# Relational layers of a graph network: groups of 20 edge tiles with 6 picked, through a ring of six one-hot pieces

## The chip, the core and the metric

The kernel runs on one core of one Trainium2 chip. The metric is the device time of one execution in microseconds. Most executions of one kernel agree within 0.3%.

## The reference, cut to what matters

Four layers of a graph network run one after the other on 3125 nodes of 32 features and 53125 edges that are sorted by destination. The change touches the first, which is two relational layers in a row. Each edge has one of 20 types, and the weights of a type are a mixture of 8 basis matrices:

```python
def _rel_layer(x, src, dst, etypes, V, a, w_loop, bias, activation=None):
    W = jnp.einsum('rb,bio->rio', a, V)
    seg = dst.astype(jnp.int32) * R + etypes.astype(jnp.int32)
    agg = jax.ops.segment_sum(x[src], seg, num_segments=N * R)
    agg = agg.reshape(N, R, -1)
    h = jnp.einsum('nri,rio->no', agg, W) + x @ w_loop + bias
    if activation is not None:
        h = activation(h)
    return h
...
h = _rel_layer(x, src, dst, etypes, V1, a1, loop1, b1, activation=jax.nn.relu)
h = _rel_layer(h, src, dst, etypes, V2, a2, loop2, b2, activation=None)
...
edge_index = jnp.stack([src, dst])
h = jnp.maximum(_layernorm(x, axis=-1), 0.0)
x = x + _L0_gnn_ref(h, src, dst, edge_type_20, ...)
```

So the output of a node is the sum of the messages of its incoming edges, and the message of an edge is the source's feature row times the matrix of the edge's type. The sum layer, the flow layer and the attention layer follow.

## The kernel before

The edges lie in `T` = 440 tiles of 128 edges; all edges of a tile end in one block of 128 nodes, of which there are `NB` = 25. `add_up_pass` (L680) is called once for each relational layer; both calls are alike but for a prologue of the first, and each is called a pass here. A pass adds the messages of all tiles into `rel_acc`, which lies in PSUM, a block's 32 columns at a time. A tile is added by one matmul in fp32 (two passes of the array, so two records in a trace): the stationary operand is the tile's destination one-hot (`rel_onehot`, 128 edges by 128 nodes), the moving one its 128 messages of 32 features.

The messages of a tile come in one of two ways. **Gathered** tiles: GpSimd (POOL) issues one indirect DMA a tile (L732), which fetches 128 rows from `message_table` in HBM, where the messages of all pairs of node and type stand. **Picked** tiles are computed on the core: VectorE (DVE) compares the tiles' source numbers, a row broadcast to all partitions (`rel_sources`), with the node numbers of one block, a chunk (L795), and so makes the chunk's part of the source one-hot (`rel_source_onehot`, in bf16); TensorE (PE) multiplies these one-hots with the node features in three bf16 parts (L870) and sums over the 25 chunks, which gives the source's features (`p_rel_picked`); ScalarE (ACT) copies them to SBUF; PE multiplies them with the eight basis matrices (L897, the basis products, into `p_rel_terms`); DVE weighs the eight terms with the coefficients of the edge's type (L812, `weigh`) and adds them up (L821, `messages`); PE adds the result like a gathered tile (`picked_messages`). The coefficients come from a small matmul (L887) with a one-hot of the types (L804).

The tiles go in groups of `RG` = 11, the last `RPT` = 3 of them picked, so there are 40 groups a pass, 8 gathers a group. Nothing but the written order of the code and its semaphores sets the order of the work; every engine runs its list in order.

- PE, a group: `pick` (25 matmuls of 384 columns, L870), `gathered_messages` (8 tiles, L861), `coefficients` (L887), `picked_messages` of the group two back (L861), `basis_products` (L897).
- DVE, a group: five stretches of five chunks' comparisons of 384 columns (L795), with two or three tiles' destination one-hots (L782) between them, then `weigh` of the group two back (L812), `types` (L804) and `messages` of the group two back (L821). The source one-hots of a whole group have two buffers, so DVE starts group g when PE has picked group g-2.
- POOL: the gathers, with six groups of row buffers; group g waits until PE has added group g-6.
- SP: the broadcasts of source and type numbers of the picked tiles (L755), six groups ahead.

## Time and profile before

| | us |
|---|---|
| median of 3 runs (lowest, highest) | 3623.91 (3616.06, 3626.77) |
| the profiled execution | 3605.4 |
| its span | 3603.6 |
| first pass, PE's first pick to its last matmul | 651.65 to 1102.4 |
| second pass, DVE's first comparison to PE's last matmul | 1176.4 to 1630.9 |
| TensorE's granted clock over the span, share of full | 0.807 |

A profile shows for each engine when it was busy, and for each idle stretch what ended it (the releaser). "issue" as a releaser means that the engine waited for nothing that the profile shows: POOL spends about 0.30 us so between two gathers. The granted clock is the share of its full 2.4 GHz that TensorE's clock had in a stretch; a single stretch has either 1.0 or 0.5 (1.2 GHz), and a mean over longer windows lies between. "PEld" is the load of a stationary operand, which goes beside the matmuls.

### The profile page before, as it was taken

To read this page: it belongs to the slowest core of one execution; us is meant where nothing else is said; L and a number is where in the kernel's file an instruction comes from. 1 tells how busy PE (TensorE), PEld (TensorE's weight loads), DVE (VectorE), ACT (ScalarE), POOL (GpSimd) and SP (SyncE) were. 2 spreads that over 40 slices of the span, in tenths; PEclk is the share of its full clock that TensorE was granted. 3 is DMA by queue.
4 is the path that set the end of the run, shared out by engine and by line. 5 is a ranking of instruction groups with operands and counts; after the bars stand their busy time and mean duration, and the time that the engine had idled before them with its cause. 6 is when DMAs were issued, how large, how long until landed. Compare 5 with 4: busy or idle time off the path is not lost. (4 is left out here: it accounts for less than half of the span.)

```text
span 3603.6 us, 57390 instructions
## 1 busy us (share of the span) xinstructions
PE 2602.2 (72%) x19362; PEld 1786.6 (50%) x19499; DVE 2548.7 (71%) x7445; ACT 576.6 (16%) x1352; POOL 2289.0 (64%) x2253
## 2 busy tenths in 40 slices
PE   0600000899998999996999799999999967777761
PEld 0300000777775777774666466666666544333331
DVE  9400000988983988878999777777777659999987
ACT  0100000000001000000111122222222213333320
POOL 2777776877770777775777455555555357777740
PEclk9655555778885788887999799999999969888875
DMA  6300001111113111111111100000000011111120
GB/s 97 104 8 8 8 8 58 31 22 23 24 15 100 25 23 23 23 13 29 29 29 29 13 10 10 10 10 11 10 11 10 6 24 27 27 27 27 27 18 5
DMA packets 125024, 91.60 MB, mean 25 GB/s; under 512 B 59542, under 2 KB 110678, under 8 KB 124118
## 3 DMA queue, kind: packets, MB, share of 16 engines
q0 software_dynamic: 70912, 41.10, 9.2%
q1 hardware_dynamic: 53846, 46.89, 5.7%
q8 instruction: 174, 2.85, 0.3%
q14 instruction: 92, 0.75, 0.1%
HBM read 60.42 MB, written 27.41 MB: 24 GB/s over the span
## 5 line engine op out<-in xcount | busy, mean ns | idle before, releaser
L732 POOL DMA_INDIRECT rel_rows<-message_table,message_indices x640 | 716.3, 1119 | 279.2 <-issue 194.4
L1287 POOL DMA_INDIRECT flow_x<-node_table,flow_index x440 | 443.1, 1007 | 401.2 <-DVE flow_index L1302 292.2
L1425 PE MATMUL flow_acc_bwd<-flow_onehot_j,flow_by_q 128*128 128x309 bf16 (+1 forms) x2503 | 552.2, 334 | 8.9 <-issue 0.2
L795 DVE TENSOR_SCALAR rel_source_onehot<-rel_sources,node_numbers 128x384 bf16<-128x384 f16 x2000 | 508.1, 315 | 62.6 <-PE p_rel_picked L870 61.4
L393 POOL DMA_INDIRECT sorted_edges<-stage,sorted_row x416 | 404.8, 973 | 191.9 <-issue 126.5
L1653 POOL DMA_INDIRECT att_kv_rows<-kv_table,att_index x440 | 424.0, 964 | 140.6 <-issue 129.8
L870 PE MATMUL p_rel_picked<-rel_source_onehot,rel_h_parts 128*96 128x384 bf16 x2000 | 429.4, 384 | 0.4 <-DVE rel_source_onehot L795 0.4
L870 PEld LDWEIGHTS p_rel_picked<-rel_source_onehot,rel_h_parts 128*96 128x96 bf16 x2000 | 297.0, 149 | 122.1 <-issue 0.7
L664 PE MATMUL p_rel_terms<-ident,source_centred 128*128 128x128 f32 (+1 forms) x4 | 1.1, 436 | 455.8 <-DVE source_centred L650 455.8
L1036 POOL DMA_INDIRECT sum_rows<-node_table,src_indices x280 | 271.2, 968 | 85.2 <-issue 85.2
L761 DVE COPY p_rel_lanes<-iota 128x128 f32<-128x128 f32 x2 | 0.6, 294 | 440.1 <-PEq L388 437.5
L1689 DVE TENSOR_REDUCE att_tile_max<-p_att_scores 128x4 f32<-128x512 f32 x440 | 282.3, 684 | 25.5 <-PE p_att_scores L1803 21.5
L1070 DVE TENSOR_SCALAR sum_source_onehot<-sum_sources,node_numbers 128x512 bf16<-128x512 f16 x1000 | 299.3, 365 | 0.0
L1123 PE MATMUL p_sum_picked<-sum_source_onehot,sum_h_stack 128*96 128x512 bf16 x1000 | 250.5, 413 | 34.5 <-DVE sum_source_onehot L1070 33.9
L1801 PE MATMUL p_att_scores<-att_mask,identb 128*128 128x512 bf16 x440 | 197.7, 449 | 67.0 <-ACT att_parts_turned L1737 67.0
L1422 PE MATMUL flow_acc_fwd<-flow_messages,flow_onehot 128*128 128x32 bf16 x1320 | 235.1, 178 | 1.5 <-DVE flow_by_q L1330 1.5
L664 PEld LDWEIGHTS p_rel_terms<-ident,source_centred 128*128 128x128 f32 (+1 forms) x4 | 0.7, 203 | 457.1 <-DVE source_centred L650 457.1
L1315 DVE TENSOR_TENSOR flow_messages<-p_hidden,flow_b 128x256 f32<-128x256 f32 x110 | 46.7, 425 | 245.8 <-PE p_hidden L1413 245.8
L844 ACT CAST rel_picked<-p_rel_picked 96x384 bf16<-96x384 f32 x80 | 38.0, 474 | 1101.5 <-PE p_rel_picked L870 1101.5
L1330 DVE TENSOR_TENSOR flow_by_q<-flow_messages,source_q_mask 128x512 bf16<-128x512 bf16 x330 | 207.3, 681 | 0.0
L861 PE MATMUL rel_acc<-rel_rows,rel_onehot 128*128 128x32 f32 x1280 | 166.3, 287 | 54.2 <-DMA rel_rows<-message_table,message_indices 53.9
L1803 PE MATMUL p_att_scores<-att_parts_turned,att_pick 96*128 96x512 bf16 x440 | 201.5, 458 | 0.0
(286 smaller groups left out, 4979.9 us busy)
## 6 DMA issues: line engine op xcount, KB each, us to landing
message_table<-message_rows SPq DMA_DIRECT2D x50, 320.0 KB, 2.1
rel_rows<-message_table,message_indices POOLq DMA_INDIRECT x640, 2.7
rel_sources<-source_rows SPq DMA_DIRECT2D x80, 96.0 KB
flow_x<-node_table,flow_index POOLq DMA_INDIRECT x440, 2.4
att_kv_rows<-kv_table,att_index POOLq DMA_INDIRECT x440, 2.5
sorted_edges<-stage,sorted_row POOLq DMA_INDIRECT x416, 2.1
sum_sources<-source_rows SPq DMA_DIRECT2D x40, 128.0 KB, 3.2
sum_rows<-node_table,src_indices POOLq DMA_INDIRECT x280, 2.4
```

Of the source, the lines that this page charges most:

```text
L393: pool.indirect_dma_start(out=d["sorted"], out_offset=bass.IndirectOffsetOnAxis(ap=row[:, c:c + 1], axis=0), in_=stage[:, c, :], in_offset ...
L732: pool.indirect_dma_start(out=rows[b][:, t, :], out_offset=None, in_=d["messages"], in_offset=bass.IndirectOffsetOnAxis(ap=s["idx_msg"][:, ...
L795: last = dve.tensor_scalar(which[g % 2][:, c, :], srcs[b][:], s["node"][:, c:c + 1], None, ALU.is_equal)
L870: last = pe.matmul(pp[g % 2][0:3 * F, 0:RW], hs[:, c].rearrange("p k f -> p (k f)"), which[g % 2][:, c, :], start=(c == 0), stop=(c == NB ...
L1036: pool.indirect_dma_start(out=rows[b][:, t, :], out_offset=None, in_=d["nodes"], in_offset=bass.IndirectOffsetOnAxis(ap=s["idx_src"][:, g ...
L1070: last = dve.tensor_scalar(which[g % 2][:, c, :], srcs[g % bufs][:], node[:, c:c + 1], None, ALU.is_equal)
L1123: last = pe.matmul(pp[g % 2][0:3 * F, 0:PT * P], hs[:, c].rearrange("p k f -> p (k f)"), which[g % 2][:, c, :], start=(c == 0), stop=(c == ...
L1287: pool.indirect_dma_start(out=X[b][:, t, 0:F], out_offset=None, in_=d["nodes"], in_offset=bass.IndirectOffsetOnAxis(ap=ibuf[b][:, t:t + 1] ...
L1422: pe.matmul(accF[:, bass.ds(cols[b, t], F)], hot[b][:, t, :], top(M[b][:])[:, k, t, 0:F], start=False, stop=True, skip_group_check=True)
L1425: last = pe.matmul(accB[:, lo:hi], S[b][:, t, k, :], J[b][:, t, lo:hi], start=False, stop=True, skip_group_check=True)
L1653: pool.indirect_dma_start(out=KV[b][:, t, :], out_offset=None, in_=d["kv"], in_offset=bass.IndirectOffsetOnAxis(ap=ibuf[b][:, t:t + 1], ax ...
L1689: dve.tensor_reduce(tm[b][:, 0, t, :], pR[t % PR][:].rearrange("p (h e) -> p h e", h=HEADS), AX_X, ALU.max).then_inc(max_ready, 1)
```

## The change

The groups become 20 tiles, 6 of them picked (22 groups a pass, 14 gathers a group; 308 gathered and 132 picked tiles instead of 320 and 120). One comparison now makes a chunk's one-hots of all six picked tiles, 768 columns. The source one-hots of a group no longer lie in one of two large buffers but go through a ring of six pieces (`SLOTS`) of five chunks each (`PIECE`), a fifth of a group. PE picks piece by piece, two matmuls of 384 columns for each chunk with the same stationary operand, into two PSUM buffers that are the two halves (`HALF` = 3 tiles) of the group. Basis products, weighing and adding up go half by half. Row buffers are 3 of 14 tiles instead of 6 of 8. The order on PE and DVE is written anew: all that PE does for a group besides picking (additions, basis products) now stands one group later, between the five picks of the next group, and DVE's `weigh` and `messages` stand one group later, after the second and the fourth piece.

```diff
-RG, RPT, RBUFS = 11, 3, 6
+RG, RPT, RBUFS = 20, 6, 3
+HALF = RPT // 2
...
+PIECE, SLOTS = NB // FIFTHS, 6
...
-            which = [sb(st1, f"{name}_source_onehot{b}", [P, NB, RW], BF16) for b in range(2)]
+            which = [sb(st1, f"{name}_source_onehot{b}", [P, PIECE, RW], BF16) for b in range(SLOTS)]
...
-            gT = [sb(st1, f"{name}_picked{b}", [3 * F, RW], BF16) for b in range(2)]
+            gT = [sb(st1, f"{name}_picked{b}", [3 * F, HALF * P], BF16) for b in range(2)]
...
-            terms = sb(st1, f"{name}_terms", [P, RPT, F, NBASIS])
-            msg = [sb(st1, f"{name}_messages{b}", [P, RPT, F]) for b in range(2)]
+            terms = sb(st1, f"{name}_terms", [P, HALF, F, NBASIS])
+            msg = [sb(st1, f"{name}_messages{b}", [P, HALF, F]) for b in range(2)]
...
+                    def sources(g, n):
+                        piece = g * FIFTHS + n
+                        if n == 0:
+                            dve.wait_ge(edge_in[g % RBUFS], 32 * (g // RBUFS) + 32)
+                        if piece >= SLOTS:
+                            dve.wait_ge(piece_used, piece - SLOTS + 1)
+                        for c in range(PIECE):
+                            last = dve.tensor_scalar(which[piece % SLOTS][:, c, :], srcs[g % RBUFS][:],
+                                                     s["node"][:, n * PIECE + c:n * PIECE + c + 1], None, ALU.is_equal)
+                        last.then_inc(piece_ready, 1)
...
+                    def weigh(g, x):
+                        dve.wait_ge(z_done, 2 * g + x + 1)
                         dve.wait_ge(coef_taken, g + 1)
+                        if g + x >= 1:
+                            dve.wait_ge(msg_ready, 2 * g + x)
...
-                    for g in range(RGROUPS):
+                    for g in range(RGROUPS + 1):
                         for n in range(FIFTHS):
-                            sources(g, n * NB // FIFTHS, (n + 1) * NB // FIFTHS)
-                            if n < FIFTHS - 1:
+                            if g < RGROUPS:
+                                sources(g, n)
+                            if n in (1, 3) and g >= 1:
+                                weigh(g - 1, n // 2)
+                            if n < FIFTHS - 1 and g < RGROUPS:
                                 onehots(g, n * RG // (FIFTHS - 1), (n + 1) * RG // (FIFTHS - 1))
-                        if g >= 2:
-                            weigh(g - 2)
-                        types(g)
-                        if g >= 2:
-                            messages(g - 2)
...
+                            if n in (1, 3) and g >= 1:
+                                messages(g - 1, n // 2)
+                            if n == 2 and g < RGROUPS:
+                                types(g)
...
+                    def pick(g, n):
+                        piece = g * FIFTHS + n
+                        pe.wait_ge(piece_ready, piece + 1)
+                        if n == 0 and g >= 1:
+                            pe.wait_ge(pick_taken, 2 * g)
+                        for c in range(PIECE):
+                            for x in range(2):
+                                last = pe.matmul(pp[x][0:3 * F, 0:HALF * P],
+                                                 hs[:, n * PIECE + c].rearrange("p k f -> p (k f)"),
+                                                 which[piece % SLOTS][:, c, x * HALF * P:(x + 1) * HALF * P],
+                                                 start=(n + c == 0), stop=(n * PIECE + c == NB - 1))
+                        last.then_inc(piece_used, 1)
...
-                    for g in range(RGROUPS):
-                        pick(g)
-                        gathered_messages(g)
-                        coefficients(g)
+                    for g in range(RGROUPS + 2):
+                        now, before = g < RGROUPS, 1 <= g <= RGROUPS
                         if g >= 2:
                             picked_messages(g - 2)
-                        basis_products(g)
-                    picked_messages(RGROUPS - 2)
-                    picked_messages(RGROUPS - 1)
+                        if before:
+                            columns(g - 1)
+                            gathered_messages(g - 1, 0, RGT // 2)
+                        if now:
+                            pick(g, 0)
+                        if before:
+                            basis_products(g - 1, 0)
+                        if now:
+                            pick(g, 1)
+                            pick(g, 2)
+                        if before:
+                            basis_products(g - 1, 1)
+                        if now:
+                            pick(g, 3)
+                            coefficients(g)
+                        if before:
+                            gathered_messages(g - 1, RGT // 2, RGT)
+                        if now:
+                            pick(g, 4)
```

PE's list, before, from the picks of one group to those of the next (`rel1_moved5` is the landing of the gathers; rows of the same addition are left out):

```order
L870 MATMUL p_rel_picked<-rel_source_onehot,rel_h_parts 96x384 [waits rel1_pick_taken,rel1_source_onehot_ready]
L870 MATMUL p_rel_picked<-rel_source_onehot,rel_h_parts 96x384 x24
L860 ISA [waits rel1_moved5,rel1_onehot_ready]
...
L887 MATMUL p_rel_coef<-rel_type_coef,rel_type_onehot 128x8 [waits rel1_coef_taken,rel1_type_onehot_ready]
L887 MATMUL p_rel_coef<-rel_type_coef,rel_type_onehot 128x8 x2
L860 ISA [waits rel1_messages_ready]
...
L897 MATMUL p_rel_terms<-rel_basis_parts,rel_picked 128x256 [waits rel1_terms_taken,rel1_pick_taken]
L897 MATMUL p_rel_terms<-rel_basis_parts,rel_picked 128x256 x8
L84 TENSOR_LOAD dst_columns
```

PE's list now, from the second pick of a group to the last additions of the group before (`rel1_source_onehot_ready` counts pieces, `rel1_terms_taken` DVE's weighings):

```order
L871 MATMUL p_rel_picked<-rel_source_onehot,rel_h_parts 96x384 [waits rel1_source_onehot_ready]
L871 MATMUL p_rel_picked<-rel_source_onehot,rel_h_parts 96x384 x9
L871 MATMUL p_rel_picked<-rel_source_onehot,rel_h_parts 96x384 [waits rel1_source_onehot_ready]
L871 MATMUL p_rel_picked<-rel_source_onehot,rel_h_parts 96x384 x9
L901 MATMUL p_rel_terms<-rel_basis_parts,rel_picked 128x256 [waits rel1_terms_taken,rel1_pick_taken]
L901 MATMUL p_rel_terms<-rel_basis_parts,rel_picked 128x256 x8
L871 MATMUL p_rel_picked<-rel_source_onehot,rel_h_parts 96x384 [waits rel1_source_onehot_ready]
L871 MATMUL p_rel_picked<-rel_source_onehot,rel_h_parts 96x384 x9
L891 MATMUL p_rel_coef<-rel_type_coef,rel_type_onehot 128x8 [waits rel1_coef_taken,rel1_type_onehot_ready]
L891 MATMUL p_rel_coef<-rel_type_coef,rel_type_onehot 128x8 x5
L860 ISA [waits rel1_moved0,rel1_onehot_ready]
```

The picks stood in one block with one wait ahead of them; now each fifth has its own wait, and basis products and additions stand between the fifths.

DVE's list, before, the end of a group and the start of the next:

```order
L795 TENSOR_SCALAR rel_source_onehot<-rel_sources,node_numbers 128x384 x5
L812 TENSOR_TENSOR rel_terms<-p_rel_terms,rel_coef 128x768 [waits rel1_messages_ready,rel1_coef_taken,rel1_terms_done]
L804 TENSOR_SCALAR rel_type_onehot<-rel_types,lane_number 20x384 [waits rel1_coef_done,rel1_edge_rows_in4]
L821 TENSOR_REDUCE rel_messages<-rel_terms 128x96 [waits rel1_used,rel1_terms_taken]
L795 TENSOR_SCALAR rel_source_onehot<-rel_sources,node_numbers 128x384 [waits rel1_pick_done,rel1_edge_rows_in5]
```

DVE's list now, from the second piece of a group to its third and the fourth:

```order
L796 TENSOR_SCALAR rel_source_onehot<-rel_sources,node_numbers 128x768 [waits rel1_source_onehot_used]
L796 TENSOR_SCALAR rel_source_onehot<-rel_sources,node_numbers 128x768 x4
L811 TENSOR_TENSOR rel_terms<-p_rel_terms,rel_coef 128x768 [waits rel1_messages_ready,rel1_coef_taken,rel1_terms_done]
L783 TENSOR_TENSOR rel_onehot<-p_rel_lanes,dst_in_block 128x640
L820 TENSOR_REDUCE rel_messages<-rel_terms 128x96 [waits rel1_used,rel1_terms_taken]
L796 TENSOR_SCALAR rel_source_onehot<-rel_sources,node_numbers 128x768 [waits rel1_source_onehot_used]
L796 TENSOR_SCALAR rel_source_onehot<-rel_sources,node_numbers 128x768 x4
L783 TENSOR_TENSOR rel_onehot<-p_rel_lanes,dst_in_block 128x640
L803 TENSOR_SCALAR rel_type_onehot<-rel_types,lane_number 20x768 [waits rel1_coef_done]
```

The weighing, which waits for PE's basis products (`rel1_terms_done`), stood behind all of a group's comparisons; now it stands twice among them, and the third piece is made behind the first of the two.

## Rows read from the trace of the kernel before

**Rows 1.** The stretches of the two passes: busy time by engine, granted clock.

```profile
core 0: us, PE busy (x) PEld busy (x) DVE busy (x) ACT busy (x) POOL busy (x), PEclk, DMA share, GB/s
643.00:1097.00 454.00, 425.86 (x2502) 344.74 (x2503) 394.60 (x1278) 26.10 (x80) 349.09 (x305) 0.80 0.17 22
1182.00:1631.00 449.00, 420.36 (x2468) 337.70 (x2466) 381.40 (x1236) 26.11 (x80) 337.76 (x308) 0.80 0.16 21
```

**Rows 2.** Who waited for whom in the first pass: total us, times, longest.

```profile
POOL rel_rows L732 <- issue: 93.6, 307, 0.3
DVE rel_terms L812 <- PE p_rel_terms L897: 34.8, 7, 15.1
...
PE rel_acc L861 <- DMA rel_rows<-message_table,message_indices: 27.2, 13, 4.0
DVE rel_source_onehot L795 <- PE p_rel_picked L870: 25.6, 11, 3.9
```

**Rows 3.** Costliest groups of the whole page: busy us, mean ns | idle before.

```profile
L732 POOL DMA_INDIRECT rel_rows<-message_table,message_indices x640 | 716.3, 1119 | 279.2 <-issue 194.4
L1287 POOL DMA_INDIRECT flow_x<-node_table,flow_index x440 | 443.1, 1007 | 401.2 <-DVE flow_index L1302 292.2
...
L1036 POOL DMA_INDIRECT sum_rows<-node_table,src_indices x280 | 271.2, 968 | 85.2 <-issue 85.2
```

**Rows 4.** PE in order of time, picks at full clock: start, us, operation, count.

```profile
1187.57 4.23 PE L870 MATMUL p_rel_picked<-rel_source_onehot,rel_h_parts 128*96 128x384 bf16 x25
1191.64 1.87 PE L861 MATMUL rel_acc<-rel_rows,rel_onehot 128*128 128x32 f32 x16
```

**Rows 5.** PE in order of time, the small matmuls between two groups of picks.

```profile
1249.40 1.87 PE L861 MATMUL rel_acc<-rel_rows,rel_onehot 128*128 128x32 f32 x16
1251.20 0.83 PE L887 MATMUL p_rel_coef<-rel_type_coef,rel_type_onehot 20*128 20x8 f32 x6
1251.96 0.86 PE L861 MATMUL rel_acc<-rel_messages,rel_onehot 128*128 128x32 f32 x6
1252.65 1.25 PE L897 MATMUL p_rel_terms<-rel_basis_parts,rel_picked 96*128 96x256 bf16 x9
1253.69 2.77 PE L870 MATMUL p_rel_picked<-rel_source_onehot,rel_h_parts 128*96 128x384 bf16 x8
```

**Rows 6.** PE in order of time, additions after a wait for gathers.

```profile
1216.25 3.62 PE L861 MATMUL rel_acc<-rel_rows,rel_onehot 128*128 128x32 f32 x16 [4.13 <-DMA rel_rows<-message_table,message_indices]
```

**Rows 7.** Granted clock in three stretches; columns as in the first group.

```profile
1209.30:1226.30 17.00, 12.87 (x62) 10.57 (x61) 15.71 (x51) 0.65 (x2) 13.65 (x12) 0.70 0.11 17
1226.30:1236.50 10.20, 10.20 (x65) 8.30 (x64) 7.33 (x26) 0.65 (x2) 7.76 (x9) 0.83 0.21 26
1236.60:1243.30 6.70, 6.70 (x52) 5.88 (x51) 6.70 (x22) 0.65 (x2) 5.18 (x6) 1.00 0.23 29
```

**Rows 8.** DVE and POOL in order of time, one group of the second pass.

```profile
1411.97 0.54 DVE L782 TENSOR_TENSOR rel_onehot<-p_rel_lanes,dst_in_block 128x384 f32<-128x384 f32 x1
1412.44 1.22 DVE L795 TENSOR_SCALAR rel_source_onehot<-rel_sources,node_numbers 128x384 bf16<-128x384 f16 x5
1412.71 1.76 POOL L732 DMA_INDIRECT rel_rows<-message_table,message_indices  x1 [0.30 <-issue]
1413.58 0.94 DVE L812 TENSOR_TENSOR rel_terms<-p_rel_terms,rel_coef 128x768 f32<-128x768 f32 x1
1414.45 0.40 DVE L804 TENSOR_SCALAR rel_type_onehot<-rel_types,lane_number 20x384 f32<-20x384 f16 x1
1414.77 0.93 DVE L821 TENSOR_REDUCE rel_messages<-rel_terms 128x96 f32<-128x768 f32 x1
```

**Rows 9.** Three comparisons: duration min/median/max ns, first and last start, forms.

```profile
L795 DVE TENSOR_SCALAR rel_source_onehot<-rel_sources,node_numbers x2000: 294/306/550, 643.4 to 1601.7; 128x384 bf16<-128x384 f16 x182
L1070 DVE TENSOR_SCALAR sum_source_onehot<-sum_sources,node_numbers x1000: 332/341/551, 1649.8 to 2005.4; 128x512 bf16<-128x512 f16 x167
L1309 DVE TENSOR_SCALAR flow_onehot_j<-iota_j,source_j x440: 419/430/614, 2045.9 to 2859.0; 128x821 bf16<-128x821 f16 x147
```

97 lines of the change are left out of this document (35 added, 62 removed).

## The prediction, written before the changed kernel had run

> **What bounds the kernel now.** I read the busy time of the two passes first [rows 1]. In each pass of some 450 us PE is busy 94% of the time, DVE 85 to 87%, POOL 75 to 77%; ACT does not matter. But busy shares mislead twice here. POOL's share leaves out the 0.30 us between two gathers: its only idle time in the pass is that one, "issue", 307 times [rows 2], so POOL never waits for anybody. 320 gathers at a mean of 1.119 us [rows 3] and 0.30 us make 454 us, which is the length of a pass: **the gathers set the pace**. And PE's 94% is at a granted clock of 0.80. PE still waits for the gathers, 27.2 us in 13 waits, and DVE waits for PE, 25.6 us for picks and 34.8 us for basis products (15 us of it once, at the end) [rows 2]. So three engines are nearly balanced, POOL a little ahead of the others.
>
> PE's own work is best counted at full clock. From start to start of rows [rows 4, 5]: 25 picks 4.07 us (0.163 each), 8 additions 1.80, coefficients 0.76, three picked messages 0.69, basis products 1.04: **8.36 us a group**. At 0.80 that is 10.45, and 40 groups make 418; PE was busy 426 [rows 1], so small gaps add 2% (factor 1.02). With the 28 us that PE is idle it is the 454 of the row. This is the formula that I use for after: work at full clock, times 1.02, over the clock, plus idle time.
>
> The clock itself is set by what PE does. It falls after the small matmuls (few columns, 4.3 us in a row [rows 5]) and comes back in the picks: a group without a wait runs at 0.83, its picks and additions at 1.00 in between [rows 7]. Where PE also waits for gathers, 4.13 us at 1216.25, the additions after it run at half clock (3.62 us against 1.87) [rows 5, 6], and that stretch of 17 us has a mean of 0.70 [rows 7].
>
> **POOL after.** 12 gathers a pass go: 12 x 1.42 = 17 us. Beside that I expect shorter gathers. A gather in these passes can stretch far over its neighbours' length, as the one of 1.76 us that starts in a run of five comparisons and ends in the weighing behind it [rows 8]. The same gather takes 0.968 us on average beside comparisons of 512 columns, and 1.007 beside those of 821 [rows 3, 9]. The new ones have 768, between the two, so 0.99: 308 x 1.29 = 397 us instead of 454. That is a gain of 57 us a pass on the engine that bounds now, and it is what could be had, if PE and DVE can follow.
>
> The Trainium skill speaks against it: "SBUF — State Buffer", section "SBUF: two separate sides", says that VectorE in a two-port mode holds a port pair for its whole instruction and that GpSimd, which writes descriptors for its gathers through it, blocks fully. By that, comparisons twice as long would lengthen the gathers, and the sum for POOL would rise above 454 instead of falling to 397. The rows of the sum and flow layers speak against that reading; it stands below as a rival.
>
> **DVE after.** The shortest comparison takes 294 ns at 384 columns, 332 at 512, 419 at 821 [rows 9]: 0.28 ns a column, so 404 ns at 768. Five of 384 take 1.22 us [rows 8], which is a start every 0.23 us, some 65 ns less than the duration; at 768 that is 0.34 us, **1.70 us a piece**. Before: 40 x 25 x 0.23 = 230 us a pass; after: 22 x 5 x 1.70 = 187. Destination one-hots: three tiles 0.47 us from start to start [rows 8]; five, at 0.135 more a tile, 0.74; four a group. Weighing 0.87 and adding up 0.86 keep their size of three tiles and come twice a group; types 0.7 (0.32 from start to start for 384 [rows 8], about twice that for 768). A group: 8.5 + 3.0 + 3.5 + 0.7 = 15.7 us, 345 a pass, against 380 before. DVE gains 35 us a pass.
>
> **PE after.** 50 picks 8.15 us, 14 additions 3.15, coefficients 1.52, six picked messages 1.38, basis products 2.08: **16.3 us a group**, 358 a pass at full clock against 334. The two picks of a chunk use the same stationary operand; the list shows a load for each, and loads hide behind matmuls now, so nothing is gained or lost. The load of 20 column numbers now stands between picked messages and additions; before, no idle time shows where it stands [rows 5], and 1.38 us of matmuls cover it, so I take 0 and bound it at 0.4 us a group.
>
> **The new order makes a wait.** DVE's first weighing in a group stands behind two pieces and waits for PE's first basis products; behind the waiting DVE stands piece 2 of the same group. PE, once those basis products are done, has only one fifth of picks (10 x 0.163 = 1.6 us at full clock, 3.2 at half) before it needs that piece. DVE must first weigh (0.87), make one-hots (0.74), add up (0.86) and make the piece (1.70), with some 0.1 for POOL's interference and 0.4 for two semaphore hops: 4.7 us. **PE stands idle 4.7 - 1.6 = 3.1 us, or 1.5 when the picks ran at half clock; I take 2.8**, once in each of 21 groups: 59 us a pass. The ring of six pieces does not help, for it is the weighing and not the ring that holds DVE: DVE has two pieces of the group made, PE has used one. After the second basis products PE has a long list without DVE (picks, coefficients, additions, picks, messages, additions, picks, basis products: 12 us at full clock) in which DVE does its remaining 9 us and then waits some 4 to 8 us. So the two wait for each other in turns, and POOL, freed, ends up waiting for row buffers.
>
> Before, the weighing stood behind all comparisons and was two groups late, and such waits were 34.8 us a pass in all on DVE and none on PE.
>
> **The clock after.** A group has two stretches of small matmuls of 3.1 us (less than the 4.3 of before) and one idle stretch of some 3 us. Between a group without idle time, 0.83, and one with it, 0.70 [rows 7], I take the middle: **0.77**. Pass: 22 x 16.3 x 1.02 / 0.77 = 475, idle 59, and 5 for the end, where half a group more is left after the last gather: **539 us, against 454**: +85 a pass, +170 for both. Against the profiled execution's 3605.4 that is 3775. The median of the three runs, 3623.91, is 18.5 above the profiled one, so the forecast for the median is **3794**. I see no effect on the other layers.
>
> Bounds: with a clock of 0.83 and an idle time of 1.5 a pass takes 441 + 32 + 5 = 478, +24, and the kernel 3672; with 0.70, 3.1 and 0.4 for the column load, 522 + 65 + 5 + 9 = 601, +147, and 3918. Both ends need two things to go the same way, so I keep within them.
>
> **Rivals.**
> 1. *The clock stays up, and the change is faster.* The small matmuls are cut into shorter stretches between picks; for it speaks that picks restore the clock at once [rows 7]. At 1.00 a group takes 16.6 + 3.1 = 19.7 us, a pass 433 + 5 = 438, -16: 3592. It decides from a mean clock of about 0.94 (22 x 16.6 / 0.94 + 59 + 5 = 452). Against it: each group now has an idle stretch, and the one row of before with such a stretch shows 0.70. Chance 0.09.
> 2. *Gathers get longer, not shorter*, as the skill's rule on the port pair would have it. If each took the 1.76 us of the long one [rows 8], POOL would need 308 x 2.06 = 634 us a pass, it would set the pace with some 180 us more a pass, 3980. The means beside 512 and 821 columns speak against it [rows 3]. Chance 0.03.
> 3. *PE does not idle*, because DVE gets ahead after all and the wait falls where PE is busy: 475 + 5 = 480, +26 a pass, 3676. The list of the changed DVE speaks against it. Chance 0.07.
> 4. *The freed gathers and the new waits cancel*: a clock of 0.90 to 0.94. 3613 to 3635. Chance 0.03.
>
> My forecast has 0.78. The range 3690 to 3860 holds the middle of it and leaves out rival 1, 2, most of 3 and the far ends. A measurement of this kernel can tell 0.3% (11 us) from no change. Slower by more: 0.78 + 0.03 + 0.07 = 0.88; within: 0.03; faster: 0.09.
>
> **What would show it.** In the changed profile: PE waiting for `rel_source_onehot`, about 21 times 3 us a pass, where before it waited for gathers; DVE's waits for basis products, 34.8 us a pass before, up to 130 us or more; POOL with waits for `rel_rows` to be used, some 100 us a pass, and gathers near 0.99 us; comparisons near 0.40 us; a granted clock of 0.74 to 0.80 in both passes; passes of about 540 us. I would be wrong if the clock stays over 0.9 (then about no change or faster), if PE's waits for pieces are under 1 us, or if POOL still shows no wait.

## The result and the profile of the changed kernel

| | before | changed |
|---|---|---|
| median (lowest to highest), us | 3619.98 (3603.87 to 3626.77) | 3659.68 (3653.99 to 3667.53) |
| profiled execution: span, us | 3603.6 | 3661.4 |
| mean granted clock over the span | 0.807 | 0.824 |

The ratio is 1.0129, with a 95% interval of 1.0100 to 1.0158. The change is slower, as forecast, but by 40 us where 170 were forecast, and 3659.68 lies under the range 3690 to 3860.

The two profiled executions differ by 57.8 us. The first pass ends with its last addition at 1120.3 us instead of 1102.4, the second at 1676.4 instead of 1630.9, so 45.5 us are gone by then. The other 12 lie in the layers behind, whose code is the same: from the end of the second pass the profiled execution of before needs 1972.7 us, that of the changed kernel and those of experiments 1 to 4 need 1983.5 to 1987.1.

The two passes of the changed kernel, as [rows 1] has them of before (there the first stretch ends 5 us ahead of the end of its pass; stretch and length, then busy time and instructions of PE, PEld, DVE, ACT and POOL, then granted clock, DMA share and GB/s):

```profile
643.00:1121.00 478.00, 418.57 (x2682) 335.50 (x2681) 340.36 (x750) 23.11 (x66) 320.26 (x293) 0.88 0.14 21
1196.80:1677.00 480.20, 420.65 (x2644) 334.58 (x2643) 332.52 (x731) 23.11 (x66) 328.56 (x299) 0.87 0.13 20
```

PE has 24 us more work a pass (at full clock) and yet is busy 12 us less in the first pass than before (430.3 us, counted to the last addition), since its clock is 0.88, not 0.80. The loss stands in the other part of the pass: PE is idle for 59 us in place of 29. Who waited for whom in the first pass (total, times, longest), to be read beside [rows 2]:

```profile
PE p_rel_picked L871 <- DVE rel_source_onehot L796: 56.7, 21, 2.8
PE p_rel_terms L901 <- DVE rel_terms L811: 1.1, 1, 1.1
PE rel_acc L861 <- DVE rel_messages L820: 0.6, 1, 0.6
...
DVE rel_terms L811 <- PE p_rel_terms L901: 134.5, 39, 8.9
...
POOL rel_rows L733 <- issue: 87.7, 277, 1.9
POOL rel_rows L733 <- PE rel_acc L861: 36.8, 16, 6.6
```

PE no longer waits for gathers in this pass; it waits for a piece of one-hots, once in each of 21 groups. DVE waits for basis products, and POOL, which never waited before, waits for row buffers. The two groups of the page that answer to [rows 3, 9]:

```profile
L733 POOL DMA_INDIRECT rel_rows<-message_table,message_indices x616 | 674.2, 1095 | 347.5 <-issue 182.8
...
L796 DVE TENSOR_SCALAR rel_source_onehot<-rel_sources,node_numbers 128x768 bf16<-128x768 f16 x1100 | 380.1, 411 | 0.8 <-DMA rel_types<-type_rows 0.6
```

One group of the second pass in order of time (start, us, operation, count, idle time before it):

```profile
1271.22 1.50 PE L891 MATMUL p_rel_coef<-rel_type_coef,rel_type_onehot 20*128 20x8 f32 x12
...
1272.65 1.75 PE L861 MATMUL rel_acc<-rel_rows,rel_onehot 128*128 128x32 f32 x14
1274.23 1.81 PE L871 MATMUL p_rel_picked<-rel_source_onehot,rel_h_parts 128*96 128x384 bf16 x10
...
1281.37 1.79 PE L871 MATMUL p_rel_picked<-rel_source_onehot,rel_h_parts 128*96 128x384 bf16 x10
1281.57 0.96 DVE L811 TENSOR_TENSOR rel_terms<-p_rel_terms,rel_coef 128x768 f32<-128x768 f32 x1 [3.76 <-PE p_rel_terms L901]
1282.44 0.82 DVE L783 TENSOR_TENSOR rel_onehot<-p_rel_lanes,dst_in_block 128x640 f32<-128x640 f32 x1
1283.17 0.94 DVE L820 TENSOR_REDUCE rel_messages<-rel_terms 128x96 f32<-128x768 f32 x1
1284.03 1.73 DVE L796 TENSOR_SCALAR rel_source_onehot<-rel_sources,node_numbers 128x768 bf16<-128x768 f16 x5
...
1285.82 2.42 PE L871 MATMUL p_rel_picked<-rel_source_onehot,rel_h_parts 128*96 128x384 bf16 x10 [2.66 <-DVE rel_source_onehot L796]
...
1288.03 2.13 PE L901 MATMUL p_rel_terms<-rel_basis_parts,rel_picked 96*128 96x256 bf16 x9
```

DVE weighs, makes destination one-hots, adds up and only then makes the piece that PE needs; PE has run out of picks meanwhile and stands for 2.66 us. That is the wait of the forecast, step for step. The clock of the same group, in two stretches with the columns of [rows 1]:

```profile
1269.18:1285.50 16.32, 13.97 (x102) 11.62 (x100) 12.32 (x27) 1.05 (x3) 12.42 (x13) 0.98 0.16 29
1285.80:1291.20 5.40, 5.38 (x26) 3.76 (x27) 3.87 (x9) 0.00 (x0) 4.49 (x4) 0.68 0.08 11
```

For 16.3 of the group's 20.6 us, with the additions and coefficients in it, PE is at 0.98. In this group the half clock comes once, behind the idle time, and falls on picks and basis products (2.42 us for ten picks against 1.79). It isn't so in every group. In the one before, the clock also falls where PE had waited for nothing since 1240.87, and additions and picked messages run at half of it (3.17 us for 14 additions against 1.73):

```profile
1248.54 2.64 PE L871 MATMUL p_rel_picked<-rel_source_onehot,rel_h_parts 128*96 128x384 bf16 x10
1250.97 2.61 PE L861 MATMUL rel_acc<-rel_messages,rel_onehot 128*128 128x32 f32 x12
1253.40 3.17 PE L861 MATMUL rel_acc<-rel_rows,rel_onehot 128*128 128x32 f32 x14
```

### The profile page after: what moved, and what is told of

The parts are those of the page before. It is cut to its first block and busy times, and to the rows that moved or that the text cites. A ratio compares the mean times of both kernels' runs of the same rounds, so it can differ in the third digit from the quotient of the medians.

```text
span 3661.4 us, 56571 instructions
## 1 busy us (share of the span) xinstructions
PE 2594.0 (71%) x19682; PEld 1769.7 (48%) x19819; DVE 2437.9 (67%) x6381; ACT 570.5 (16%) x1324; POOL 2246.8 (61%) x2229
## 5 line engine op out<-in xcount | busy, mean ns | idle before, releaser
L733 POOL DMA_INDIRECT rel_rows<-message_table,message_indices x616 | 674.2, 1095 | 347.5 <-issue 182.8
L871 PE MATMUL p_rel_picked<-rel_source_onehot,rel_h_parts 128*96 128x384 bf16 x2200 | 460.1, 364 | 114.3 <-DVE rel_source_onehot L796 113.8
L871 PEld LDWEIGHTS p_rel_picked<-rel_source_onehot,rel_h_parts 128*96 128x96 bf16 x2200 | 287.7, 136 | 227.7 <-DVE rel_source_onehot L796 132.7
L796 DVE TENSOR_SCALAR rel_source_onehot<-rel_sources,node_numbers 128x768 bf16<-128x768 f16 x1100 | 380.1, 411 | 0.8 <-DMA rel_types<-type_rows 0.6
L1707 DVE TENSOR_REDUCE att_tile_max<-p_att_scores 128x4 f32<-128x512 f32 x440 | 283.2, 684 | 25.1 <-PE p_att_scores L1821 20.6
L811 DVE TENSOR_TENSOR rel_terms<-p_rel_terms,rel_coef 128x768 f32<-128x768 f32 x88 | 84.2, 957 | 278.6 <-PE p_rel_terms L901 278.2
L841 ACT COPY rel_coef<-p_rel_coef 128x48 f32<-128x48 f32 x44 | 8.7, 198 | 1249.0 <-PE p_rel_coef L891 1249.0
```

The source lines that it names most:

```text
L733: pool.indirect_dma_start(out=rows[b][:, t, :], out_offset=None, in_=d["messages"], in_offset=bass.IndirectOffsetOnAxis(ap=s["idx_msg"][:, ...
L796: last = dve.tensor_scalar(which[piece % SLOTS][:, c, :], srcs[g % RBUFS][:], s["node"][:, n * PIECE + c:n * PIECE + c + 1], None, ALU.is_ ...
L871: last = pe.matmul(pp[x][0:3 * F, 0:HALF * P], hs[:, n * PIECE + c].rearrange("p k f -> p (k f)"), which[piece % SLOTS][:, c, x * HALF * P ...
L1707: dve.tensor_reduce(tm[b][:, 0, t, :], pR[t % PR][:].rearrange("p (h e) -> p h e", h=HEADS), AX_X, ALU.max).then_inc(max_ready, 1)
```

## Experiments

Four kernels ran on one chip; the kernel before had a median of 3607.23 us there.

### 1. Both orders rewritten so that PE never needs a fresh piece (e1_no_idle)

The two lists stand here by the names of their calls, not as code.

```diff
 # DVE, one group: the order of the calls
-sources 0, onehots, sources 1, weigh 0, onehots, messages 0, sources 2, onehots, types,
-sources 3, weigh 1, onehots, messages 1, sources 4
+sources 0, onehots, sources 1, onehots, types, sources 2, weigh 0, onehots, messages 0,
+sources 3, onehots, weigh 1, sources 4, messages 1
 # PE, one group
-picked messages, gathered 0, pick 0, basis 0, pick 1, pick 2, basis 1, pick 3,
-coefficients, gathered 1, pick 4
+gathered 0, pick 0, basis 0, picked messages, pick 1, pick 2, coefficients, basis 1,
+pick 3, gathered 1, pick 4
```

> The changed kernel with another order on DVE and PE, same work: DVE weighs after the third and the fourth piece instead of after the second and the fourth, types stand one place earlier, and PE puts picked messages and coefficients between the picks and the second basis products. Theory A (the wait of PE for the third piece, 57 us a pass, is what the changed kernel loses): that wait falls under 10 us a pass, the passes shrink from 478 to about 440, where 308 gathers of 1.40 us (431 us) are the bound, and the kernel takes 3580 to 3605 us. Rival B (the ten per cent more picks on PE are what it loses): the idle time only moves, and the time stays within 15 us of the changed kernel's 3660.

Measured: 3582.59 us, ratio 0.9931 (0.9911 to 0.9952), as theory A had it; rival B falls. By the ratios it beats both kernels. Its passes and the waits of the first:

```profile
643.00:1081.00 438.00, 396.44 (x2687) 327.55 (x2687) 344.33 (x751) 23.14 (x66) 328.93 (x294) 0.91 0.14 23
1157.00:1597.00 440.00, 392.07 (x2645) 319.70 (x2644) 335.00 (x731) 23.14 (x66) 332.44 (x300) 0.91 0.14 22
...
PE rel_acc L878 <- DMA rel_rows<-message_table,message_indices: 41.0, 15, 6.5
...
POOL rel_rows L733 <- issue: 89.3, 293, 0.3
```

No wait for a piece is left, POOL waits for nobody, and the pass is 308 gathers x (1.12 + 0.30) = 438 us: the gathers set the pace again. So the larger groups were worth 22 us in this pass (459.4 us before, counted from 643 to the last addition, and 437.4 here), and the written order of DVE and PE hid it. What this run can't say is which of the two orders did it, nor whether the clock (0.91 for 0.88) came from the waits for pieces, which are gone, or from PE's order.

### 2. All fourteen additions in one place (e2_one_stretch)

```diff
-gathered_messages(g - 1, 0, RGT // 2)   # ahead of pick 0
 ...
-gathered_messages(g - 1, RGT // 2, RGT) # ahead of pick 3
+gathered_messages(g - 1, 0, RGT)        # behind the picked messages
```

> The changed kernel with all 14 gathered tiles of a group added in one place, right behind the picked messages, instead of in two halves. Theory C (TensorE's clock stays up in the changed kernel, 0.88 against 0.80, because the small matmuls are cut into short stretches with picks between them): the stretch of small matmuls becomes 4.5 us, the mean clock of the passes falls to 0.82 or less, PE is busy some 30 us a pass longer, and the kernel takes 3700 to 3730 us. Rival D (the clock is up because PE no longer waits for gathers right beside its small matmuls): clock 0.87 to 0.88 and the time within 15 us of 3660.

Measured: 3762.72 us, ratio 1.0436 (1.0397 to 1.0475). The first pass, its waits, and PE in one group:

```profile
643.00:1174.00 531.00, 447.22 (x2690) 353.63 (x2690) 344.72 (x752) 23.14 (x66) 313.49 (x294) 0.84 0.12 19
...
PE p_rel_picked L871 <- DVE rel_source_onehot L796: 80.2, 48, 2.9
...
DVE rel_terms L811 <- PE p_rel_terms L901: 182.4, 31, 12.6
...
1306.18 2.61 PE L861 MATMUL rel_acc<-rel_messages,rel_onehot 128*128 128x32 f32 x12
1308.60 6.16 PE L861 MATMUL rel_acc<-rel_rows,rel_onehot 128*128 128x32 f32 x28
1314.58 3.41 PE L871 MATMUL p_rel_picked<-rel_source_onehot,rel_h_parts 128*96 128x384 bf16 x10
```

In this group the same additions take 6.16 us in one row of 28 matmuls, all at half clock, where two rows of 14 take 1.75 and 1.73 at full clock in the group shown of the changed kernel. The clock of the pass fell from 0.88 to 0.84 and PE was busy 29 us a pass longer. Theory C holds in its direction, with two misses: I had expected a lower clock still, 0.82 or less, and less loss in time, 3700 to 3730 us. The time has a second part, waits on both sides that grew by 24 us (PE) and 48 us (DVE) a pass, because a long row of additions also holds up the basis products that DVE waits for.

### 3. The kernel before, with its picks cut in two (e3_before_split)

The waits stay ahead of the first part, and the signal that the picks are done stays behind the second.

```diff
-                        pick(g)
+                        pick(g, 0, 13)
                         gathered_messages(g)
+                        pick(g, 13, NB)
                         coefficients(g)
```

> The kernel before with one edit on PE: the 25 picks of a group are cut in 13 and 12, and the additions of the gathered tiles stand between them. Theory C (short stretches of small matmuls keep the clock up): the mean clock of the passes rises from 0.80 to 0.87 or more. Since gathers set the pace before (no wait on POOL), the time stays within 0.5% of before even so, and PE waits for gathers longer, 27 to 60 us a pass. Rival D: the clock stays at 0.80, since the waits for gathers stay.

Measured: 3633.19 us, ratio 1.0088 (1.0060 to 1.0115). The same stretch of this kernel and then of the kernel before:

```profile
700.00:1080.00 380.00, 334.30 (x2060) 265.73 (x2059) 329.36 (x1071) 21.54 (x66) 299.40 (x265) 0.86 0.14 21
...
700.00:1080.00 380.00, 356.78 (x2100) 287.17 (x2099) 336.06 (x1083) 22.19 (x68) 298.06 (x269) 0.81 0.15 21
```

PE has 2% fewer instructions in it and is busy 22 us (6%) less, at 0.86 in place of 0.81, since the small matmuls no longer stand in one row. PE's waits for gathers rose from 27.2 to 48.2 us a pass and the clock rose all the same. The kernel is no faster, for PE isn't what sets its pace. It is 0.9% slower, where I had expected a difference within 0.5%, and the clock missed the expected 0.87 narrowly; what costs the 26 us isn't shown (the gathers are 0.012 us longer on average, 8 us in all).

Whether idle time lowers the clock stands in the traces. The table has the time at half clock in the first pass, from its first pick to its last addition, in us and with the number of stretches. A stretch counts as behind a wait when it begins during an idle time of PE of over 0.8 us or within 2.5 us of its end.

| kernel | at half clock | behind a wait | no wait ahead |
|---|---|---|---|
| before | 178 | 101 (12) | 76 (22) |
| this one, picks cut | 123 | 116 (17) | 7 (2) |
| changed | 103 | 55 (16) | 49 (9) |
| changed, additions joined (experiment 2) | 155 | 60 (10) | 95 (20) |
| changed, both orders rewritten (experiment 1) | 69 | 66 (10) | 3 (1) |

So both lower it. Cutting the picks took away nearly all the half clock that no wait preceded (76 us, then 7; with a limit of 2.0 us, 97 and then 14), and joining the additions doubled it: that part is the order's. The other part follows waits, and it is the larger one in this kernel and in experiment 1. From the kernel before to the changed one both parts fell, so rival D of experiment 2 has a share too; how large it is depends on the limit (47 us of 75 with 2.5 us, 26 with 2.0).

### 4. The kernel before with seven gathers a group (e4_seven_gathers)

The eighth gather of a group is left out, and its tile is added up from the seventh's rows.

```diff
-                        for t in range(RGT):
+                        for t in range(RGT - 1):
                             pool.indirect_dma_start(
```

> The kernel before with work left out: seven gathers a group instead of eight, and the eighth tile is added from the rows of the seventh, so PE and DVE do the same as before. Theory G (the gathers set the pace before): 280 gathers of 1.42 us are 398 us, PE's 418 to 426 us at its clock become the bound, the passes shrink by 20 to 30 us each and the kernel takes 3560 to 3585 us. Rival (PE is the bound already): within 10 us of before.

Measured: 3548.87 us, ratio 0.9839 (0.9799 to 0.9879), 58 us less, and 11 less than the lowest that theory G had. The gathers' group, beside [rows 3]:

```profile
L732 POOL DMA_INDIRECT rel_rows<-message_table,message_indices x560 | 680.8, 1216 | 253.8 <-issue 170.1
```

POOL was busy 35.5 us less (716.3 before) and had 80 gaps of 0.30 us fewer, 24 us: 59.5 together, which is the whole gain. So the gathers did set the pace before. But 80 gathers fewer, by the 1.42 us of the forecast, should have freed 114 us. The rest became longer (1.216 us): 146 of 560 take over 1.3 us, where it was 117 of 640. DVE's comparisons come faster now, in a first pass of 419 us instead of 451, and may hold more of them; that they do isn't shown.

### 5. One order at a time, and shorter runs of comparisons

Three more kernels were to settle what was left. The first has e1's DVE order alone, the second its PE order alone, the third is e1 with one tile of destination one-hots behind each comparison of pieces 0 to 3:

```diff
                             last = dve.tensor_scalar(which[piece % SLOTS][:, c, :], srcs[g % RBUFS][:],
                                                      s["node"][:, n * PIECE + c:n * PIECE + c + 1], None, ALU.is_equal)
-                        last.then_inc(piece_ready, 1)
+                            if c == PIECE - 1:
+                                last.then_inc(piece_ready, 1)
+                            if spread:
+                                onehots(g, FIFTHS * n + c, FIFTHS * n + c + 1)
```

In all runs of this section, those of the kernel before too (medians 4253 to 4305 us), engines stood between instructions for which nothing was waited, so ratios count here only within the section, and no time is compared with the sections ahead. A trace shows it where the first pass begins (the kernel with DVE's order alone, third run):

```profile
683.93 0.42 DVE L796 TENSOR_SCALAR rel_source_onehot<-rel_sources,node_numbers 128x768 bf16<-128x768 f16 x1 [0.98 <-issue]
683.95 0.21 PE L978 MATMUL rel_acc<-w_loop,h_transposed 33*128 33x32 f32 x1 [2.59 <-issue]
...
685.33 0.42 DVE L796 TENSOR_SCALAR rel_source_onehot<-rel_sources,node_numbers 128x768 bf16<-128x768 f16 x1 [0.98 <-issue]
...
686.05 0.21 PE L978 MATMUL rel_acc<-w_loop,h_transposed 33*128 33x32 f32 x1 [1.89 <-issue]
```

A comparison starts every 1.4 us here where 0.34 is usual, a matmul every 2.1 to 2.8.

| kernel | DVE order | PE order | ratio to before, each run | clock, 730 to 1230 us |
|---|---|---|---|---|
| f1_changed | changed | changed | 1.027 | 0.80 |
| f2_both_orders | e1's | e1's | 1.000 | 0.85 |
| e6, e6b, e6c, e6d, f3 | e1's | changed | 1.003, 1.008, 0.999, 1.002, 1.010 | 0.76 (f3) |
| e7, e7b, e7c, f4 | changed | e1's | 1.062, 1.073, 1.059, 1.053 | 0.78 (f4) |
| e5, e5b, e5c | e1's, spread | e1's | 1.054, 1.059, 1.051 | |

What was expected of the first attempt:

> The reordered version (first experiment) with the destination one-hots spread: one tile of them behind each of the comparisons of pieces 0 to 3, in place of five tiles behind five comparisons. The work is the same and complete; VectorE has 16 more instructions a group. Theory H (a gather asked for while comparisons follow each other is held until their run ends, which makes the mean 1.12 us instead of 0.97): the mean gather falls to 1.00 to 1.05 us, GpSimd needs 308 x 1.33 = 410 us a pass instead of 437, the passes shorten by 15 to 25 us each as far as TensorE (393 to 396 us busy) lets them: 3535 to 3565. Rival I (the mean gather is set by VectorE's busy share, not by the length of its runs): the gather stays at 1.10 to 1.15 us, VectorE pays about 16 x 0.06 us more a group, and the time is that of the first experiment or up to 10 us above it: 3580 to 3595.

> The changed kernel with VectorE's order of the first experiment alone (the first weighing behind piece 2 and the second behind piece 3's one-hots, the adding up one step behind each); TensorE's order stays the changed kernel's. Theory A (what the changed kernel loses is the wait of TensorE for the third piece, which comes from VectorE's order): TensorE's waits for pieces fall from 57 us a pass to under 15, a pass is 430 to 445 us, the time 3580 to 3610. Rival B (TensorE's own work and clock hold the pass; the idle time only moves to other waits): over 3635. If idle time lowers the granted clock, it rises here from 0.88 towards 0.91; if only the stretches of small matmuls do, it stays at 0.88.

> The changed kernel with TensorE's order of the first experiment alone (picked messages and second half of the additions away from each other, coefficients between picks and the second basis products); VectorE's order stays the changed kernel's, with the weighing ahead of piece 2. Theory A: TensorE still waits for pieces, with picked messages (0.7 us, or 1.4 at half clock) as more cover in front of the wait: 1.5 to 2.5 us in each of 21 groups, 30 to 50 us a pass, 3620 to 3655. Rival C (the order of TensorE's work, through the clock, made the gain of the first experiment): granted clock 0.91 or above, TensorE busy under 400 us a pass, and the time under 3610. With the second run of this batch it tells what share of the granted clock the idle time has and what share the order has.

Of the second:

> The same kernel as in the experiment of short runs before this one, in which engines stood for instructions (TensorE 905 us with the waited-for work long done, against 65 in the first experiment) in the kernel before and in all three others alike. Expected where that doesn't occur: theory H (a gather is held until a run of comparisons ends): gathers 1.00 to 1.05 us, passes 15 to 25 us shorter than in the first experiment, 3535 to 3565. Rival I (the busy share of VectorE sets the gather): gather 1.10 to 1.15 us, 3580 to 3595. The disturbed run showed 0.954 us a gather, but a VectorE that stood often; it says nothing for either.

> The changed kernel with VectorE's order of the first experiment alone, once more. Theory A: TensorE's waits for pieces under 15 us a pass (57 in the changed kernel), passes of 430 to 445 us, 3580 to 3610. Rival B: over 3635. If idle time lowers the granted clock it rises from 0.88 to 0.91 here; if only the order of small matmuls and picks does, it stays at 0.88.

> The changed kernel with TensorE's order of the first experiment alone, once more; VectorE's weighing stands ahead of piece 2 as in the changed kernel. Theory A: TensorE waits 1.5 to 2.5 us for a piece in each of 21 groups, 30 to 50 us a pass, 3620 to 3655. Rival C (TensorE's order made the gain, by the clock): clock 0.91 or above and under 3610.

Of the third, and of one more run of DVE's order alone:

> The changed kernel with VectorE's order of the first experiment alone, a third time, for a run in which the engines don't stand for their instructions. Theory A: TensorE's waits for pieces under 15 us a pass (57 in the changed kernel), passes of 430 to 445 us, 3580 to 3610. Rival B: over 3635. If idle time lowers the granted clock it rises from 0.88 to 0.91 here; if only the order of small matmuls and picks does, it stays at 0.88.

> The changed kernel with TensorE's order of the first experiment alone, a third time; VectorE's weighing stands ahead of piece 2 as in the changed kernel. Theory A: TensorE waits 1.5 to 2.5 us for a piece in each of 21 groups, 30 to 50 us a pass, 3620 to 3655. Rival C (TensorE's order made the gain, by the clock): clock 0.91 or above and under 3610.

> The first experiment's version with one tile of destination one-hots behind each comparison, a third time. Theory H (a gather is held until a run of comparisons ends): gathers 1.00 to 1.05 us, passes 15 to 25 us shorter than in the first experiment, 3535 to 3565. Rival I (the busy share of VectorE sets the gather): gather 1.10 to 1.15 us, 3580 to 3595.

> The changed kernel with VectorE's order of the first experiment alone, once more, to see whether the engines still stand for their instructions. If not: theory A as before, TensorE's waits for pieces under 15 us a pass, passes of 430 to 445 us, 3580 to 3610; rival B over 3635. If they still stand: 4280 to 4320, as the kernel before.

And the batch that set the four orders side by side:

> The changed kernel itself, beside the three versions of this batch, so that the four make a square of two orders on one chip. If the engines don't stand for instructions: a ratio of 1.01. If they do: theory A (VectorE's order makes the loss) 1.04 to 1.08, near the version that has TensorE's order alone changed (1.06); rival C (TensorE's order makes it) near the version with VectorE's order alone changed, 1.00.

> The first experiment's kernel again. Without the standing: 0.993. With it: theory A 0.98 to 1.01, near the version with VectorE's order alone changed; rival C 1.05 or more below the version with VectorE's order alone, that is under 0.96.

> VectorE's order alone changed. Without the standing: theory A 0.99 to 1.00 of the kernel before, TensorE's waits for pieces under 15 us a pass; rival B over 1.005; the granted clock 0.91 if idle time lowers it, 0.88 if not. With it: 1.00 as three times before.

> TensorE's order alone changed. Without the standing: theory A 1.003 to 1.012 of the kernel before, waits for pieces of 1.5 to 2.5 us in each group; rival C under 1.000 with a clock of 0.91. With it: 1.06 as three times before.

PE's waits for pieces in both passes together, of f1, f2, f3 and f4 in this order, and below them the clock of f2 and f3 in one stretch of 500 us (columns as in [rows 1]):

```profile
PE p_rel_picked L871 <- DVE rel_source_onehot L796: 168.8, 44, 12.9
...
PE p_rel_picked L888 <- DVE rel_source_onehot L796: 44.4, 16, 8.1
...
PE p_rel_picked L888 <- DVE rel_source_onehot L796: 9.0, 14, 1.2
...
PE p_rel_picked L871 <- DVE rel_source_onehot L796: 245.3, 50, 17.6
```

```profile
730.00:1230.00 500.00, 408.10 (x2610) 329.77 (x2609) 324.90 (x704) 22.92 (x65) 294.83 (x266) 0.85 0.11 18
...
730.00:1230.00 500.00, 458.72 (x2562) 367.17 (x2562) 319.74 (x698) 23.21 (x66) 289.44 (x266) 0.76 0.11 18
```

In time, none of these met what was expected without the standing, nor could it. Of what was expected with it, f2's 0.98 to 1.01 came; f3 and f4 have 1.010 and 1.053 where 1.00 and 1.06 were expected, and e6d took 4260.66 us, under its 4280 to 4320, as the kernel before did (4253.39). What can be read from them lies in waits, clocks and durations.

*Which order.* DVE's alone takes the waits for pieces from 168.8 to 9.0 us. What that is worth in time is less sure: on one chip the ratio goes from 1.027 (1.020 to 1.034) to 1.010 (1.000 to 1.020), and the four runs on other chips have 0.999 to 1.008. Under e1's PE order it is plain, 1.053 without DVE's order and 1.000 with it. PE's order alone makes waits and ratio worse, 245.3 us and 1.05 to 1.07, against rival C. f1 came in under its 1.04 to 1.08, nearer to the kernels with DVE's order than theory A had it.

*The clock.* From f1 to f3 the waits for pieces go (PE busy 402 of 500 us, then 459) and the clock doesn't rise: 0.80, then 0.76. From f3 to f2 PE's own order changes and it goes from 0.76 to 0.85. From f1 to f4 the same change of PE's order, under the old DVE order, takes it from 0.80 to 0.78, so the order of PE isn't all of it. About idle time these runs say little, since PE also stands for late instructions: behind idle times of over 0.8 us lie 140 of the 242 us at half clock in f1's first pass, and 140 of the 251 in f3's. The table under experiment 3 weighs more; but in none of its undisturbed kernels does one of e1's two orders stand alone.

*The gathers.* Durations in ns (min/median/max) of f1 and of e5c, and a stretch of e5c:

```profile
L733 POOL DMA_INDIRECT rel_rows<-message_table,message_indices x616: 938/944/3718, 653.7 to 1905.6; - x154
...
L733 POOL DMA_INDIRECT rel_rows<-message_table,message_indices x616: 941/947/2360, 654.1 to 2030.9; - x154
...
1101.28 0.28 DVE L783 TENSOR_TENSOR rel_onehot<-p_rel_lanes,dst_in_block 128x128 f32<-128x128 f32 x1
1101.40 0.94 POOL L733 DMA_INDIRECT rel_rows<-message_table,message_indices  x1 [11.37 <-PE rel_acc L873]
1101.48 0.41 DVE L796 TENSOR_SCALAR rel_source_onehot<-rel_sources,node_numbers 128x768 bf16<-128x768 f16 x1
1101.80 0.28 DVE L783 TENSOR_TENSOR rel_onehot<-p_rel_lanes,dst_in_block 128x128 f32<-128x128 f32 x1
```

The median gather takes 0.94 to 0.95 us in every kernel but that of experiment 4 (1.00); the mean is made by a few long ones. In e5c, counted from the trace, 2 of 616 take over 1.3 us, in f1 75 and in f2 61, and the means are 0.953, 1.079 and 1.108 us. DVE's instructions come late in all three, so the closest comparison is that of gathers which start in the same instruction, the type one-hot (L803 in f1): in f1 and f2 five comparisons follow it, in e5c one. The 17 gathers of f1 that start there have a mean of 2.30 us, the 22 of f2 one of 2.66, the 23 of e5c one of 0.948. The undisturbed changed kernel says the same from the other end: of its 63 gathers over 1.3 us, 62 end 0.1 to 0.8 us behind the last comparison of a run. So it is the unbroken run that holds a gather, not the single comparison; theory H stands (even beyond its 1.00 to 1.05), rival I falls. Not every gather beside a run is held: of the 205 of the changed kernel that start in a comparison of source numbers, 182 take under 1.3 us. What picks out the others isn't shown.

The spread version is slower here than e1's kernel (1.05 against 1.000), though its gathers are shorter. It has 704 DVE instructions more, and DVE's come slowly; that these cost the time isn't shown. Whether it is the fastest on an undisturbed chip is open. By an estimate from these runs, its bound would be 308 x 1.25 = 386 us for POOL, and PE's 358 x 1.02 / 0.91 = 401 us would then be the longer.

## Why the prediction missed

The direction was right, and so was its reason. The size was not. By its steps:

- *The gathers set the pace before*: right. Experiment 4 gained 58 us, which is what POOL's time lost.
- *PE's idle time, 2.8 us in each of 21 groups, 59 us a pass*: right. 56.7 us in 21 waits of at most 2.8. That DVE's order is its cause is shown by f3, where the waits went with it. The chain that was put at 4.7 us took 4.3 in the group shown, from the end of the basis products at 1281.53 to the pick at 1285.82; no row shows the 0.4 for two semaphore hops, and by the trace's ends the two gaps there are 0.04 and 0.06 us.
- *DVE, 404 ns a comparison, 1.70 us a piece, 345 us a pass*: right. 411 ns, 1.72 us and 340 us busy. Its waits for basis products, forecast up to 130 us or more, were 134.5.
- *PE's work, 358 us a pass at full clock, times 1.02*: right. 358 x 1.02 / 0.88 = 415 us, and PE was busy 418.6.
- *The clock, 0.77, "the middle" between 0.83 and 0.70*: **this step failed**. It was 0.88. The mis-sized term is 358 x 1.02 / 0.77 = 474 us, where it measured 419: 56 us a pass, 112 of the 130 by which the total was off. I took the clock of two groups of before [rows 7] as that of a group with and without idle time, and both carried more than that. Both have one row of small matmuls of 4.3 us [rows 5]; in the changed kernel the longest, coefficients and additions from 1271.22 to 1274.23, takes 3.0, and experiments 2 and 3 show what such rows do to the clock (0.88 to 0.84 when the additions are joined, 0.81 to 0.86 when the picks are cut). And the 0.70 is of a group that waited for gathers right ahead of its small matmuls, which then ran at half clock for 10 us:

```profile
1216.25:1226.30 10.05, 10.05 (x44) 8.70 (x45) 8.77 (x30) 0.18 (x1) 7.92 (x8) 0.50 0.14 21
```

Behind a wait for a piece stand picks and basis products, and the 5.4 us behind it are at 0.68 as a whole. So a wait cost less clock than in [rows 7]: 101 us at half clock behind 12 waits before, 55 behind 16 in the changed kernel. Whether that comes from the work behind the wait or from the waits' length isn't separated. Rival 1 named the first half of this and got 0.09; its own condition, 0.94, wasn't met.
- *Gathers of 0.99 us*: wrong, 1.095. I put 768 columns between 512 and 821 on a scale of lengths [rows 3, 9]; runs, not lengths, matter (*The gathers* above). A gather that is asked for just ahead of a run can wait it out, as here in the changed kernel, where the run of five comparisons goes from 1286.94 to 1288.66:

```profile
1286.88 2.28 POOL L733 DMA_INDIRECT rel_rows<-message_table,message_indices  x1 [0.30 <-issue]
```

The error cost no time there, since POOL had room: it waited 36.8 us for row buffers, not the 100 of the forecast. It does in experiment 1, where 0.1 us a gather is 31 us a pass. The rule of the Trainium skill that I had as rival 2 ("SBUF — State Buffer", section "SBUF: two separate sides": GpSimd's descriptor writes are shut out for the whole of a two-port VectorE instruction) is nearer to this than my rows were, though no run shows in which mode the comparisons go; what the traces add is that a gather can be held over several instructions, and that it isn't with one tile of another operation behind each (e5c).
- *The end, +5 us*, and no effect on other layers: right, as far as the passes' sum (478 against 415 + 57 + 5 = 477) and the stages behind show, which took in the changed kernel what they took in experiments 1 to 4.
- *Rival 4, "a clock of 0.90 to 0.94: 3613 to 3635"*: its sum doesn't come out. By the formula a clock of 0.90 gives 22 x 16.6 / 0.90 + 59 + 5 = 470 us a pass, and 3656.

With the clock and the waits as measured the forecast's own formula gives 477 us a pass, 23 more than its 454, and 3670 for the median, 10 above the result.

## What to carry to other kernels

When work on PE is made larger and cut up differently, don't carry a mean clock over from one group to another: look at what PE did ahead of each stretch at half clock. Here long rows of small matmuls and waits each had a share, and cutting the rows took away the one (76 us, then 7) and not the other. Where two engines hand work to each other, a ring of buffers is worth nothing if the consumer's next piece stands behind an instruction that waits for the consumer; put the weighing behind the piece (with PE's order changed to match, 1.0129 became 0.9931 here). And gathers that GpSimd issues beside VectorE's comparisons should be costed by the length of the unbroken runs, not by that of one instruction.

## What the hardware showed that I had not expected

- A gather of a median of 0.944 us can take 3.7 us when it starts just ahead of a run of comparisons of 128 x 768 (one of ten in the longest case), and takes 0.95 us where a one-hot of another operation stands behind each.
- In the five undisturbed kernels of the table TensorE stood at half clock for 69 to 178 us of a first pass of 428 to 521 us, partly behind waits of 1 to 7 us and partly in work without any wait.
- Leaving out one gather in eight made the others 9% longer on average (1.216 us against 1.119), so nearly half of the expected gain was lost.
- The same chip ran the kernel before in 3607 us and later in 4286 us. In the second case DVE's and PE's instructions started 1.4 to 2.8 us apart in stretches, for no visible cause; operations kept their durations. I did not find out what delays them.
